# Turns, the values of the double slot before, and scores in one TensorE stretch

## The reference

```
# 1: windowed attention, 16 heads of 32, queries from x, keys and values = ctx
q = layernorm(x)
scores = (qh @ kh^T) / sqrt(32);  -inf where |query - key| > 64
x = x + softmax(scores) @ vh @ W_proj^T + b_proj
# 2: a gated cell scanned over the 8 batches, 512 positions side by side
y = layernorm(x)
step(c, y_b): f = sigmoid(y_b wf^T + c uf^T + bf);  i = sigmoid(y_b wi^T + c ui^T + bi)
              g = tanh(y_b wc^T + c uc^T + bc);     c = f*c + i*g
x = x + tanh(y @ wo^T + c_final @ uo^T + bo)
```

## Time and profile before

| | |
|---|---|
| median of 3 runs | 938.56 us (938.07 to 938.91) |
| the profiled execution | 939.05 us, its span 937.2 us |
| TensorE matmuls busy | 920.3 us, 98% of the span |
| VectorE busy | 674.9 us, 72% |
| ScalarE busy | 476.7 us, 51% |
| GpSimd busy | 206.0 us, 22% |

### The profile page before, as it was taken

How to read it: one execution, slowest core, us unless ns; L and a number is a source line. 1 busy time by engine, 2 the same in 40 slices (tenths; PEclk the granted TensorE clock), 3 DMA queues, 4 the chain that set the end, 5 groups by cost and what they waited for, 6 DMA issues and landing times.

```text
span 937.2 us, 21983 instructions
## 1 busy us (share of the span) xinstructions
PE 920.3 (98%) x7842; PEld 716.2 (76%) x7842; DVE 674.9 (72%) x2275; ACT 476.7 (51%) x1430; POOL 206.0 (22%) x236
## 2 busy tenths in 40 slices
PE   7999899999999999999999999999999999999998
PEld 5555567677887788878787888788877888888887
DVE  6888987888779977997799878987798531143222
ACT  6888666655555544555465555555555321131222
POOL 5576322211111111111111111111101100003444
PEclk9999999999999999999999999999999999999999
DMA  9564223224443443434543444344333150059862
GB/s 303 165 200 145 86 80 108 87 69 130 132 139 112 130 132 92 143 108 129 133 141 109 119 116 125 108 109 109 98 99 92 50 164 0 1 178 384 316 233 101
DMA packets 139348, 123.58 MB, mean 132 GB/s; under 512 B 46824, under 2 KB 104168, under 8 KB 137704
## 3 DMA queue, kind: packets, MB, share of 16 engines
q1 hardware_dynamic: 138520, 121.91, 42.9%
q10 hardware_dynamic: 720, 0.27, 0.2%
HBM read 87.70 MB, written 34.46 MB: 130 GB/s over the span
## 4 chain that ended last, share of the span: by engine, by line
PE 89%; DVE 5%; ACT 2%; issue 2%; DMA 1%; SPq 0%; DVEq 0%; ACTq 0%
PE ps_g L706 18%; PE ps_g L708 18%; PE ps_g L707 18%; PE ps_a L753 5%; PE ps_a L775 5%; PE ps_m L706 3%; PE ps_v L796 3%; PE ps_m L708 3%; PE ps_m L707 3%; PE ps_m L828 2%; PE ps_a L708 2%; PE ps_a L706 2%; PE ps_a L707 2%; ACT probs L923 2%; PE ps_v L801 2%
## 5 line engine op out<-in xcount | busy, mean ns | idle before, releaser
L923 ACT ACTIVATE probs<-probs,rowmin 128x192 f32<-128x192 f32 (+1 forms) x512 | 239.4, 470 | 114.0 <-DVE rowmin L1035 114.0
L1035 DVE CUSTOM_DVE_ANT_0 probs<-ps_a,mask 128x192 f32<-128x192 f32 (+1 forms) x512 | 166.1, 386 | 28.4 <-PE ps_a L753 26.8
L706 PE MATMUL ps_g<-state_hi,gate_w 128*128 128x512 f32 x336 | 133.6, 398 | 0.0
L708 PE MATMUL ps_g<-state_hi,gate_w 128*128 128x512 f32 x336 | 131.1, 390 | 0.0
L707 PE MATMUL ps_g<-state_lo,gate_w 128*128 128x512 f32 x336 | 130.8, 389 | 0.0
L1070 DVE STREAM_TRANSPOSE keys<-probs 32x128 f32<-32x128 f32 x420 | 125.5, 299 | 5.6 <-issue 0.2
L970 ACT ACTIVATE gate<-ps_g,bias 128x512 f32<-128x512 f32 x84 | 57.6, 686 | 105.8 <-PE ps_g L708 105.1
L923 ACT ACTIVATION_READ_ACCUMULATOR probs<-probs,rowmin 128x1 f32 x512 | 96.4, 188 | 0.0
L928 ACT ACTIVATE probs_t<-ps_a 128x512 f32<-128x512 f32 x108 | 59.3, 595 | 61.1 <-PE ps_a L775 61.1
L685 POOL TENSOR_TENSOR attn_lo<-recip,attn_hi 128x512 fp32r<-128x512 f32 x23 | 29.7, 1292 | 275.8 <-ACT attn_hi L936 275.8
L706 PE MATMUL ps_g<-x2t_even,gate_w 128*128 128x512 f32 x192 | 80.5, 419 | 0.0
(11 more groups left out here) (220 smaller groups left out, 1723.5 us busy)
## 6 DMA issues: line engine op xcount, KB each, us to landing
values<-ctx_rows SPq DMA_DIRECT2D x34, 256.0 KB, 4.4
xr<-x SPq DMA_DIRECT2D x32, 256.0 KB, 3.8
keys<-ctx_t SPq DMA_DIRECT2D x16, 512.0 KB, 4.2
x_dram<-xr SPq DMA_DIRECT2D x32, 256.0 KB, 2.6
gate_w<-x2t_dram SPq DMA_DIRECT2D x8, 1024.0 KB, 10.1
keys<-ctx_t SPq DMA_DIRECT2D x16, 384.0 KB, 3.4
x2t_dram<-x2t_even SPq DMA_DIRECT2D x12, 512.0 KB, 4.4
x2t_dram<-x2t_odd SPq DMA_DIRECT2D x12, 512.0 KB, 4.5
```

The costliest lines, as they stand in the source:

```text
L706: pe.matmul(ps, lhs[0], rhs[0], start=start, stop=False)
L708: return pe.matmul(ps, lhs[1], rhs[0], start=False, stop=stop)
L923: act.activation(row, row, ACT.Exp, bias=rowmin[:, i % 2, h:h + 1], scale=-1.0, accum_out=rowsum[:, i // G % 2, i % G, h:h + 1]).then_inc( ...
L1035: dve.tensor_tensor_reduce(probs[:, i % 2, h, 0:SEEN[t]], ps_a[h][:, score_at[i]:score_at[i] + SEEN[t]], mask[:, MASK0[t]:MASK0[t] + SEEN[ ...
```

## The change

In the double slots the order is rewritten, with three edits that follow from it. TensorE first makes both turns, then the values of the *preceding* double slot (n-2, n-1), then the scores of n+2 and n+3, and after that all cells. Before, it made the turns, two cells, the scores, the values of n and n+1, then the other cells. `mult` and `halves` of tile i-1 move with the values to the s = 0 double slot; `proj` follows five cells later. The `sides` of slots n and n+1 stand in the double slot n, ahead of the masks, and not in the one before. The masks become a step of their own. The turns of odd slots go to ps_m, which the projection and other transposes use too, and so wait for those. Copies wait only for the values of their own half; scores wait only for the copy of the even slot. `turn2_hi` moves, for most tiles, from the end of the s = 0 double slot behind the two copies of the next.

```diff
             steps.extend(("turn", m) for m in both)
-            if s == 0:
-                tile_steps("ln1", i + 2)
+            steps.extend(("value", m) for m in back)
+            steps.extend(("score", m) for m in ahead)
+            if s == 0 and i - 1 >= SENT:
+                tile_steps("mult", i - 1)
+                tile_steps("halves", i - 1)
+            if s == 2 and i - 2 in MOVED and i - 1 in MOVED:
+                tile_steps("turn2_hi", i - 2)
+            late_sides = [m for m in both if m >= FIRST_TWO + 2]
+            steps.extend(("sides", m) for m in late_sides[:1])
             cells(2)
...
             gates(2)
-            steps.extend(("score", m) for m in ahead[:1])
+            steps.extend(("sides", m) for m in late_sides[1:])
...
-            steps.extend(("score", m) for m in ahead[1:])
+            steps.extend(("mask", m) for m in ahead)
...
             steps.extend(("exp", m) for m in ahead)
-            steps.extend(("value", m) for m in both)
-            if s == 0:
-                tile_steps("proj", i - 1)
-            else:
-                tile_steps("mult", i)
             gates()
             renew()
             cells(3)
...
             if s == 0:
+                tile_steps("proj", i - 1)
+            gates()
+            if s == 0:
+                tile_steps("ln1", i + 2)
+                steps.extend(("recip", m) for m in ahead)
...
-        ps_turn = [... ps_a[n % 2 if n >= FIRST_TWO else 0] ...]
+        ps_turn = [... ps_m if n >= FIRST_TWO and n % 2 else ps_a[0] ...]
...
-                        pe.wait_ge(turned_a, i - i % 2)
+                        pe.wait_ge(turned_a, i - i % 2 - 1)
...
+                        if i % 2:
+                            pe.wait_ge(recip_out, SENT)
+                            pe.wait_ge(x1_done, tile - 1 + (i % G) // 2)
+                            pe.wait_ge(x2_lo, split_by(tile - 1))
+                            pe.wait_ge(q_ready, min(tile + 1 + (i % G) // 2, TURNED_X))
...
-                    need(act, valued, i - i % 2 if i >= FIRST_TWO else i)
+                    need(act, valued, i - 1 if i >= FIRST_TWO + 2 else i - i % 2 if i >= FIRST_TWO else i)
```

More of the change, by code:

```diff
@@ L169, in bass_xattn_ffn @@
             ahead = [m for m in (n + 2, n + 3) if m < SLOTS]
+            back = [m for m in (n - 2, n - 1) if FIRST_TWO <= m < SLOTS]
             steps.extend(("turn", m) for m in both)
-            if s == 0:
-                tile_steps("ln1", i + 2)
+            steps.extend(("value", m) for m in back)
[7 more added lines that the diff above has]
+            steps.extend(("sides", m) for m in late_sides[:1])
             cells(2)
@@ L200, in bass_xattn_ffn @@
             cells(3)
-            steps.extend(("recip", m) for m in ahead[:1])
             if s == 0:
+                tile_steps("proj", i - 1)
[3 more added lines that the diff above has]
+                steps.extend(("recip", m) for m in ahead)
                 tile_steps("resid", i - 1)
                 tile_steps("stat2", i - 1)
[L205 to L208, removed]
                 tile_steps("send", i)
-            steps.extend(("sides", m) for m in ahead[:1])
             if s == 0 and i + 1 >= TURNED_X:
                 tile_steps("query_norm", i + 1)
+            if s == 0 and i - 2 in MOVED:
+                tile_steps("turn2", i - 2)
+                if i - 1 not in MOVED:
+                    tile_steps("turn2_hi", i - 2)
+            gates()
+            cells(7)
             if s == 0 and i + 1 < TURNED_X:
@@ L215, in bass_xattn_ffn @@
                 tile_steps("query_out", i + 1)
[L216 to L220, removed]
             if s == 0 and i - 1 not in MOVED:
@@ L233, in bass_xattn_ffn @@
             gates(3)
-            steps.extend(("sides", m) for m in ahead[1:])
+            if s == 2:
+                steps.extend(("recip", m) for m in ahead)
             renew()
@@ L486, in bass_xattn_ffn @@
         x2t_home[0] = x2t_home[B - 2]
-        ps_turn = [ps_g[0] if n < OWN_BANKS else ps_a[n % 2 if n >= FIRST_TWO else 0] for n in range(SLOTS)]
+        ps_turn = [ps_g[0] if n < OWN_BANKS else ps_m if n >= FIRST_TWO and n % 2 else ps_a[0] for n in range(SLOTS)]
         sides_t = keys[:, 1].rearrange("p g k -> p (g k)").rearrange("p (h q) -> p h q", q=P)
@@ L769, in _ @@
                     if i >= FIRST_TWO:
+                        tile = i // G
                         pe.wait_ge(masked, HPG * (i - i % 2 + 2))
+                        if i % 2:
[3 more added lines that the diff above has]
+                            pe.wait_ge(q_ready, min(tile + 1 + (i % G) // 2, TURNED_X))
                     else:
@@ L833, in _ @@
                             pe.wait_ge(q_ready, min(i + 2, TURNED_X))
+                            pe.wait_ge(turned_a, min(G * (i + 1) + 2, SLOTS))
                         for k in range(G):
@@ L841, in _ @@
                     need(pe, column_turned, len([n for n in row_at if n < G * (i + 1) + 2]))
+                    if i + 1 >= SENT:
+                        pe.wait_ge(turned_a, min(G * (i + 1) + 4, SLOTS))
                     for k in range(G):
@@ L1027, in _ @@
                     dve.tensor_tensor(queries[:, :, :], queries[:, :, :], rstd, ALU.mult).then_inc(q_ready, 1)
-                if kind == "score":
+                if kind == ("mask" if isinstance(i, int) and i >= FIRST_TWO + 2 else "score"):
                     t = i // G % TT
@@ L1059, in _ @@
                     dve.wait_ge(expd, HPG * (i + 1))
-                    dve.wait_ge(valued, i - i % 2 if i >= FIRST_TWO else i)
+                    dve.wait_ge(valued, i - 1 if i >= FIRST_TWO + 2 else i - i % 2 if i >= FIRST_TWO else i)
                     if i == OWN_BANKS:
```

## The result

The changed kernel takes 962.14 us, the median of 4 runs (960.88 to 962.74), beside 938.32 us for the kernel before in the same session (937.71 to 938.91): a ratio of 1.0252, 95% interval 1.0234 to 1.027. The forecast was 960.7 us, 950 to 970. The profiled execution took 962.52 us, its span is 960.6 us, 23.4 more than before.

The account below looks back on a forecast made before the run. TensorE, busy 610 of 610 us, was taken as the bound. Span 937.2 + 19.7 (scores' wait) + 2.4 (queries) = 959.3, + 1.85 around it = 961.15, less 0.49 for the median: 960.7 us, range 950 to 970.

Parts of the forecast that it names:

- The bound and the wait: TensorE waits for nobody before; after, scores wait for ScalarE's copy behind the values of n-2, 0.44 wide, 0.55 us narrow.
- The price of a double slot: TensorE, first turn to next cell: 3.24 us wide, 3.13 narrow, so 0.37 and 0.52 us more; 19.7 us in sum.
- The handover from the values to the copy: ScalarE's copy starts about 0.05 us after the values of n-2 end on TensorE.
- the scores with their switch: On TensorE, scores plus the switch out of them take 0.81 us per double slot.
- The give-back: One switch between kinds of matmul fewer on TensorE gives back 0.00 to 0.14 us per double slot.
- The queries: Scores at t = 1 wait for VectorE's late query_norm: 0.4 us in each of 6 tiles, 2.4 us, ends 0 and 8.
- what is carried into the double slot of n = 84: Blends and states carried into that double slot lengthen VectorE's queue ahead of query_norm by 0.2 to 0.7 us.
- The 0.7 us for the sums: VectorE's queue ahead of query_norm grows 0.7 us because the sums wait for exps that end later.
- `turn2_hi` and the odd turn: ScalarE's turn2_hi hides behind the copies and the odd turn's new waits in ps_m are met: both cost nothing.
- VectorE did not become the bound: Rival: late exps make turns wait in some 12 tiles with t = 1 and 2, 12 to 24 us more; chance 0.11.
- The clock did not fall: Rival: the hole between turns and next cell brings half clock, 77 us more, 1036 us; chance 0.03.
- The faster side: Rival: TensorE's stretch 0.15 us shorter in 45 double slots with the copy hidden, 7 us less, 932 us; chance 0.05.

Follow-up runs that it names:

- e2: Changed kernel with values reading a constant row instead of copied probabilities, so the copy need not wait for them; own-key weighting left out, timing only: 941.48 us.
- e5: Changed kernel with the values of n-1 moved behind the scores: 985.49 us.
- e1: Changed kernel with two cells put between the values and the scores: 947.61 us.
- e10: Changed kernel with query_norm directly behind the residual on VectorE, nothing left out: 960.90 us.
- e6: Kernel of e2 with query_norm moved ahead of the layernorm statistics, the sums and the residual on VectorE: 979.89 us.
- e9: Kernel of e2 with query_norm moved between residual and statistics on VectorE: 944.64 us, 939.04 to 948.93 in 12 runs.

## Why the prediction was right

**The bound and the wait: right.** TensorE's stream had no wait; it now has 45, released by the copy. Predicted start of the scores 2.43 and 2.32 us after the first turn, measured 2.47 and 2.37. The predicted stall, 0.44 and 0.55 us, is the delay of the scores' start; measured in this way, against e2, it is 0.50 and 0.61. The profile's idle times of 0.43 and 0.54 us look like a closer hit, but they are another quantity. The steps of the chain are shown by e2 (take the copy's wait away: no hole), e5 (take the cover away: the scores start at the same time) and e1 (fill the hole: it is gone).

**The price of a double slot: a little small.** The forecast put the next cell at 3.24 and 3.13 us, and so 0.37 and 0.52 us more than before. It is at 3.31 and 3.21. Two terms were too small. The handover from the values to the copy takes 0.13 us (507.19 to 507.32), where the forecast had 0.05 from turns; the values start 0.02 earlier than forecast, which takes back a little. And the scores with their switch were taken as 0.81 us from one wide double slot; they take 0.84 in the narrow ones and in half of the wide ones. The difference per double slot is 0.44 and 0.60, in sum 24 x 0.44 + 20 x 0.60 + 0.4 = 23 us in place of 19.7. The give-back of 0.03 to 0.07 us that the forecast allowed for the switches is in this, and e2 bears it out.

**The queries: the one step that failed.** The forecast added 2.4 us for scores that wait for `query_norm` at t = 1, s = 2. Nothing of it was lost. It did take the later of the two waits, since it set the scores at 2.4 us; what it had wrong is when VectorE is done. VectorE ends there at 507.50, 1.91 us after the first turn, where I had 2.1 to 2.6:

```profile
506.81 0.69 DVE L1040 TENSOR_TENSOR queries<-queries,tile_row 128x512 f32<-128x512 f32 x1
```

The step that was mis-sized is what is carried into the double slot of n = 84: the forecast added 0.2 to 0.7 us for blends and states there. The blend that took 1.66 us at 479.09 takes 0.69 in the changed kernel, and the state is blended 1.19 us after the first turn where it was 1.42:

```profile
491.13 0.69 DVE L1169 SCALAR_TENSOR_TENSOR gate<-gate,state 128x512 f32<-128x512 f32 x1 [2.34 <-ACT gate L983]
491.86 0.69 DVE L1172 SCALAR_TENSOR_TENSOR state<-gate 128x512 f32<-128x512 f32 x1
```

The 0.7 us for the sums came about (VectorE idles 0.62 us for the exps). With the end at 1.91 the queries are ready about 0.5 us before the copy lets the scores go, and e10 shows that still earlier gains nothing. Only where the copy's wait was taken away did this one come out, five times 0.4 us (e2).

**The sum: luck in part.** The double slots from n = 38 to 124 took 24.8 us more than before, where the forecast had 19.3 without the queries. That every double slot is dearer than forecast is most of the gap; three late copies (1.2 us) and one wait of an odd turn (0.6 us), both below, are the rest. Against that, the 2.4 us for the queries were not lost, and outside these double slots the span is 1.4 us shorter, which the forecast did not have: the double slot of n = 36 takes 14.79 us in place of 16.71, since it does no values and two of its waits are gone; the part before it is 0.5 shorter, and the end, where the last values now stand, 1.0 longer. Before n = 36 the traces also differ by their clock: half clock from 115.2 to 118.6 us, and none in the changed kernel. So errors of both signs nearly cancelled, and the total was closer than its parts.

**`turn2_hi` and the odd turn: taken at nothing, not quite.** In three double slots (n = 50, 82, 114) the wait is 0.82, 1.03 and 1.00 us and not 0.54, 1.2 us in sum. There t = 0, and `turn2_hi` is still ahead of the copies; it is so too at n = 66 and 98, where nothing is late. The engines at n = 82, whose first turn is at 478.89:

```profile
476.75 1.77 POOL L674 TENSOR_TENSOR xr<-xr,bp_row 128x512 f32<-128x512 f32 x1
...
477.41 1.66 DVE L1040 TENSOR_TENSOR queries<-queries,tile_row 128x512 f32<-128x512 f32 x1
...
479.18 0.71 DVE L1124 STREAM_TRANSPOSE tile_row<-x2t_even 128x512 f32<-128x512 f32 x1
...
479.92 0.63 ACT L958 ACTIVATE x2t_even<-tile_row 128x512 fp32r<-128x512 f32 x1 [6.07 <-DVE tile_row L1124]
...
481.03 0.59 ACT L941 ACTIVATE probs_t<-ps_a 128x512 f32<-128x512 f32 x1
...
481.76 0.91 PE L757 MATMUL ps_a<-keys,queries 32*64 32x192 f32 x32 [1.03 <-ACT probs_t L941]
```

GpSimd's addition and VectorE's 477.41 piece overlap, and that piece takes 1.66 us in place of 0.69; transpose, high half, gate and copy follow one behind the other. That the overlap is what makes it long is argued from such pairs in the trace and was not tried. Nor does it account for all three: in e10 that piece takes 0.69 us at n = 82 and the scores start at 2.37 like others, but they still start at 2.74 at n = 114 behind pieces of 0.69, and at n = 50 these pieces take no longer than elsewhere in the changed kernel either. What makes the copy late there stays open. And at n = 38 the first odd turn waited once for the queries of the last tile that TensorE turns, since both now use ps_m:

```profile
192.86 0.59 ACT L925 ACTIVATE queries<-ps_m 128x512 f32<-128x512 f32 x1
...
193.70 0.63 PE L785 MATMUL ps_m<-ident,probs 128*128 128x128 f32 x4 [0.59 <-ACT queries L925]
```

**The rivals.** VectorE did not become the bound: no turn waited for an exp past n = 36. The clock did not fall: it is 1.00 from 250 to 860 us with a hole of half a microsecond in every double slot. The Trainium skill (TensorE: Matmul & The Clock Gate, Part 4: PE-mode transpose) has transposes not counted as busy in the same way; here 2.5 us of transposes, small matmuls and idle time at a stretch took nothing off the clock. With longer idle time it did fall: in e6, where TensorE was busy for 0.94 of the 3.44 us before 379.94, and once in e9, behind a wait of 2.5 us (0.50 from 674.5 to 677.9). The faster side had 0.05, for a stream 0.15 us shorter with the copy hidden; e2 has the copy hidden, its stream is 0.13 us shorter in one kind of double slot at most, and it is 3 us slower than the kernel before.

## What to carry over

When a step is moved ahead of another on the bound engine, look for a third engine that must work between the two, and lay out its chain from the first instruction that really releases it; the cover is only what the bound engine has left to do after that release, here one slot's values (0.45 us) for a copy that takes 0.6 and two handovers. Compare a forecast stall with the delay of the start, and not with the idle time of the profile, which is counted from a modelled end and was 0.07 us less here. Waits that stand before the same instruction do not add up: take the latest, as e2 and e10 show. And an edit that is worth nothing in one order (a ScalarE piece out of the way of a copy) may be worth something in another, so it is timed in the order in which it will run.

## What the hardware showed

- The switch from one kind of matmul to another had the same price in either order: values with the switch behind them took 1.01 us before cells and 1.01 us before scores. Merging two stretches into one gave back 0.01 us in a narrow double slot and up to 0.13 in a wide one (e2 beside the kernel before), too little to see in the total.
- A handover taken from a trace holds for the rows it was read from: 0.13 us from the modelled end of the values to the copy (507.19 to 507.32), beside 0.03 from that of turns to the copy in rows 7; 0.14 from the copy to the scores (507.92 to 508.06). The forecast had 0.05 for the first, taken from turns, and 0.16 for the second.
- A wait of half a microsecond in every 11 to 14 us left the granted clock at 1.00. Where TensorE was busy for 0.94 of 3.44 us (e6), half clock followed.
